# A two-layer graph attention block with a routed FFN: edge counting moved beside the first projection

## The chip, the cores and the metric

The kernel runs on one core of one Trainium2 chip. The metric is the device time of one execution in microseconds (us). Before the change the median of three runs is 1415.3 us (1413.14 to 1418.47).

## The reference, cut to what matters

```python
# x [1250, 768]; src, dst [21250], dst ascending (20000 drawn edges and 1250 self loops)
def gat(x, src, dst, W, a_src, a_dst, bias, concat):
    h = (x @ W).reshape(N, H, C)                     # layer 1: H=4, C=512; layer 2: H=1, C=768
    al_s, al_d = einsum('nhc,hc->nh', h, a_src), einsum('nhc,hc->nh', h, a_dst)
    e = leaky_relu(al_s[src] + al_d[dst], 0.2)
    ex = exp(e - segment_max(e, dst)[dst])
    alpha = ex / segment_sum(ex, dst)[dst]
    out = segment_sum(h[src] * alpha[:, :, None], dst)
    return (out.reshape(N, H * C) if concat else out.mean(axis=1)) + bias
# src, dst are the given edges followed by one more self loop per node
x = x + gat(elu(gat(layernorm(x), W1, ...)), W2, ...)
x = x + routed_ffn(layernorm(x))                     # 8 experts, top 2, and a shared expert
```

## The kernel before, in words

**Numbers.** Products are made in f16 pairs: every operand is split into a high half (ScalarE copies it to f16) and a low half (VectorE subtracts), and TensorE makes three matmuls for each product (`mm3`, L1692: high by high, high by low, low by high).

**Tiles.** The 1250 nodes are ten tiles of 125. The graph is turned into a dense matrix of counts CT [source in tile, source tile, destination], f16, built by matmuls: the 21250 edges are 170 tiles of 125; for each of them a one-hot of the source's place within its tile (OL, 125 wide) is multiplied with a one-hot of the pair of source tile and destination within a chunk of 50 destinations (OR, 500 wide, or 1000 where the tile meets two chunks). `reach[c]` is the range of edge tiles that chunk c is summed over and `met[t]` the one or two chunks that tile t meets. Since dst is ascending, a tile meets few chunks; that all edges were inside the ranges is checked at run time, and a general path, every tile by every chunk, runs if they weren't.

**Stages before the attention.** Each engine has its own program, and semaphores order them.

1. SyncE loads edges, x in three pieces (L485), W1 for head 0 (L487), a column of biases (L489), and the attention vectors (L500, L501). VectorE makes keys out of the edges (L1155 to L1161), TensorE transposes them (L1700), VectorE copies them to KEY and SLO (L1166, L1167).
2. `piece` (L1187): for a piece of x VectorE makes mean and variance (`norm`, L1174 to L1185, ScalarE the square root at L863) and normalises each tile (L1192). TensorE transposes a tile (`x_T`, L1709) into one of two pairs of banks, ScalarE and VectorE make its halves (L901, L1220), and SyncE stores them (L509), for there are three slots for ten tiles. During this stage W1's halves (L882, L1198) and the first 24 edge tiles are done. For each edge tile ScalarE subtracts (L870), VectorE compares 18 of them at once to give OL (L1229), makes OR (L1236; a ring of 8), and TensorE counts (L1722).
3. First projection, `proj(0)` on TensorE: ten tiles, beginning with tile 7 (`x_tile`), because the last three are still in their slots; the others are reloaded (L522). ScalarE makes the high half of h (`h_hi`, L888) and subtracts for more edge tiles, VectorE makes the two attention sums (L1208, twice) and the low half (L1213), and part of the 32 sums of W2's rows with the second layer's attention vectors (`v2_sums`, L1261).
4. The other 146 edge tiles. ScalarE keeps each finished chunk with its sum (L917, through four banks). Then the sum of all counts is compared with the number of edges (L1287, L1771, L1289, and a register load on VectorE and TensorE), and self loops are added to CT (L1307, L1310).
5. Masks for each of ten destination tiles: ten transposes (L1791), a scaled Relu (L1000), a store (L602), and the maximum over the sources (`chain_max`, L1331), with three tiles of the second head's projection between. `chain_shift` (L1337 to L1341) and `chain_shift_rows` (L1346) turn the maxima into rows that are stored and loaded again, broadcast.
6. The other seven tiles of the second head's projection, beside the first steps of head 0's P. A step is one source tile by one of three blocks of destinations (500, 375 and 375 wide), and takes ScalarE L929, L935, L947 and VectorE L1352, L1360, L1367; there are 30 per head.

**Attention.** A head has 15 groups: for each block the denominators (L1815) and four channel groups of 30 matmuls (L1820) in a ring of four banks. VectorE reads a group (L1405), ScalarE makes the elu's parts (L972, L973), VectorE the rest (L1412), and both the halves of H1 (L984, L1420). `al2` (L1835) sums 12 rows over a finished block. Lists say how much other work lies in each group: `CUR_STEPS` and `NEXT_STEPS` the steps of P, `PJ_STEPS` those beside the next projection, `MAX_STEPS` the maxima, `w2_at` the halves of W2's 16 chunks (L992, L1425): eight of them lie in the last head, one for each of its last eight groups, and the rest behind it, beside the second layer's first projection tile, whose matmuls wait chunk by chunk. W2's chunks come through three slots, each reloaded once its low half is made.

Of the kernel before, what the change touches and what calls it, by code (L numbers as in the profile page):

```python
# [34 lines left out]
def build(nc, x, src, dst, W1, as1, ad1, b1, W2, as2, ad2, b2, Wr, w1, w3, w2, s1, s3, s2, out):  # L35
# [33 lines left out]
    NC = N // DC  # L69
    MARGIN = 250  # L70
    KC = NT * DC
    SP = 512
    KA = ET + 1
    assert ET % 2 == 0 and KC <= SP
    reach = [(max(0, c * DC * NE // N - MARGIN) // T, min(ET, -(-((c + 1) * DC * NE // N + MARGIN) // T)))
             for c in range(NC)]
    met = [[c for c in range(NC) if reach[c][0] <= t < reach[c][1]] for t in range(ET)]
# [5 lines left out]
    XF = PIECES[2][0]  # L83
    T0 = 24
    assert T0 <= min(2 * OLP, reach[4][0])

# [11 lines left out]
    OL = at(o_p, [T, KA, T], F16)  # L98
# [32 lines left out]
    W1F = at(o_ct, [128, KD, C], F32)  # L131
    BS1 = at(o_ct + 12288, [T, NT, 2, 6], F32)
    MV1 = at(o_ct + 12800, [T, NT, 2], F32)
    WV = [at(o_y + 3072 * b, [128, D], F32) for b in range(6)]
    A2R = at(o_y + 18432, [128, 2, D], F32)
    VJ = at(o_y + 24576, [128, D], F32)
    assert o_y + 27648 <= o
# [56 lines left out]
    KEY = at(o_k + 2304, [T, KA], F32)  # L194
    SLO = at(o_k + 3072, [T, KA], F32)
# [14 lines left out]
    CS = small([T, NC], F32)  # L210
# [48 lines left out]
    with ctx:  # L259
# [26 lines left out]
        s_keys = sem("keys_made")  # L286
        s_var = sem("variance_made")
        s_sd = sem("deviation_made")
        s_xn = sem("x_normalised")
# [14 lines left out]
        s_slo = sem("sources_in_tile_made")  # L304
        s_od = sem("source_differences_made")
        s_ce = sem("chunk_kept")
        s_cs = sem("count_sum_steps")
# [5 lines left out]
        s_ctok = sem("counts_final")  # L313
# [107 lines left out]
        def v2_in(ch):  # L421

            return (s_w2g + s_wv)[ch % 6], 16 * (ch // 6 + 1)

        def x_tile(h, q):

            return (Q0 + q) % NT if h == 0 else q

        def x_use(h, q):

            return Q0 + NT * h + q

        def max_row(h):

            return ROWM[:, :] if 0 < h < H else ROW[:, 0, :]
# [10 lines left out]
        PJ_STEPS = [[0, 0, 0, 0, 2, 2, 2, 2, 2, 2], [1] * NT, [1] * NT]  # L446
# [33 lines left out]
        def _(sp):  # L480
# [49 lines left out]
            for i in range(NT):  # L530
                store_xt(i)
# [1541 lines left out]
```

## Time and profile before

| | |
|---|---|
| median of three runs | 1415.3 us |
| the profiled execution | 1416.0 us |
| its span | 1414.2 us |
| TensorE busy, share of the span | 1249.2 us, 88% |
| VectorE busy | 895.3 us, 63% |
| ScalarE busy | 604.5 us, 43% |
| GpSimd busy | 162.4 us, 11% |
| mean granted TensorE clock | 0.939 |
| data moved by DMA | 151.56 MB, 107 GB/s |
| first VectorE instruction, after waiting for the edges | 4.82 us |
| issue of W1 for head 0 | 4.42 us |
| first transpose for a mask | 197.43 us |
| last group of head 3, end of its matmuls | 724.9 us |

The times inside the span run from its start. An execution's own time has a small part around the span, 1.8 us here. The granted clock is a share of full speed (1.00 is 2.4 GHz, 0.50 is 1.2 GHz). A busy engine is one with an instruction in it; it need not run at its peak.

### The profile page before, as it was taken

Reading aid. Unit: us, or ns where it says so; the run is one execution under the profiler, and the core shown is the slowest. Engines: PE = TensorE matmul, PEld = TensorE weight load, DVE = VectorE, ACT = ScalarE, POOL = GpSimd, SP = SyncE. Lnnn points to the kernel's source line nnn. Section 1 sums busy time; section 2 is a strip of 40 time slices with the busy share of each in tenths; the row PEclk is TensorE's granted clock in tenths of the full one; section 3 lists DMA queues with packets and bytes.
Section 4 is the critical chain, followed back from the end, with each engine's and each line's share of the span. In section 5 each row is a group of like instructions: output and inputs, shape, how many; then the busy total and the mean of one; then the engine's idle time right before and its main releaser. Section 6 shows DMA issues by size and latency. Waiting matters only on the chain.

```text
span 1414.2 us, 18321 instructions
## 1 busy us (share of the span) xinstructions
PE 1249.2 (88%) x7084; PEld 816.2 (58%) x7084; DVE 895.3 (63%) x1764; ACT 604.5 (43%) x1122; POOL 162.4 (11%) x144
## 2 busy tenths in 40 slices
PE   3773987678799899989989999999999889999996
PEld 2441554334454455444557888888854756666664
DVE  6675987898987898789854556244577623333340
ACT  4275233555743574278731355000331134444441
POOL 1000000000000000000000000500010644444422
PEclk9796998898899899999998999999799989999999
DMA  8443015133413531330165410611400277767622
GB/s 205 164 137 128 23 56 164 28 101 107 122 55 101 136 99 50 90 103 23 52 207 164 141 59 30 179 63 34 138 19 1 75 237 190 190 175 180 168 61 30
DMA packets 71010, 151.56 MB, mean 107 GB/s; under 512 B 10789, under 2 KB 34853, under 8 KB 70298
## 3 DMA queue, kind: packets, MB, share of 16 engines
q1 hardware_dynamic: 64267, 133.13, 31.3%
q0 software_dynamic: 6656, 17.26, 6.3%
q8 instruction: 56, 0.92, 0.3%
q14 instruction: 31, 0.25, 0.1%
HBM read 117.78 MB, written 34.59 MB: 108 GB/s over the span
## 4 chain that ended last, share of the span: by engine, by line
PE 56%; DVE 20%; ACT 9%; issue 5%; DMA 5%; SPq 2%; POOL 2%; POOLq 0%; DVEq 0%; ACTq 0%
PE PS L1692 42%; PE PS L1820 9%; DVE sb L1236 3%; DVE sb L1331 3%; ACT sb L870 3%; DVE sb L1352 2%; DMA sb<-aa_d 2%; PE PS L1815 2%; DVE sb L1208 1%; DVE sb L1261 1%; SPq L500 1%; DVE sb L1367 1%; DMA sb<-in_L_gnn_W_dram 1%; DVE sb L1360 1%; DVE sb L1405 1%
## 5 line engine op out<-in xcount | busy, mean ns | idle before, releaser
L1692 PE MATMUL PS<-sb,sb 128*125 128x384 f16 (+8 forms) x4404 | 789.4, 340 | 47.1 <-DVE sb L1213 25.2
L1692 PEld LDWEIGHTS PS<-sb,sb 128*125 128x125 f16 (+3 forms) x4404 | 545.4, 130 | 277.9 <-issue 62.9
L1820 PE MATMUL PS<-sb,sb 125*128 125x375 f16 (+1 forms) x1440 | 267.0, 347 | 0.0
L1820 PEld LDWEIGHTS PS<-sb,sb 125*128 125x128 f16 x1440 | 141.9, 99 | 122.4 <-issue 13.8
L935 ACT ACTIVATE sb<-sb 125x375 f32<-125x375 f32 (+1 forms) x150 | 81.5, 544 | 125.0 <-DVE sb L1352 124.6
L1536 DVE SCALAR_TENSOR_TENSOR sb<-sb,sb 128x2304 f16<-128x2304 f32 x27 | 68.8, 2557 | 87.8 <-ACT sb L1067 87.8
L778 POOL TENSOR_TENSOR sb<-sb,sb 125x768 f32<-125x768 f32 x10 | 18.0, 1838 | 895.0 <-DMA sb<-in_x_dram 895.0
L1352 DVE SCALAR_TENSOR_TENSOR sb<-sb,sb,sb 125x375 f32<-125x375 f32 (+1 forms) x150 | 95.3, 637 | 11.3 <-ACT sb L929 11.3
L929 ACT ACTIVATE sb<-sb,sb 125x375 f32<-125x375 f32 (+1 forms) x150 | 93.7, 628 | 7.7 <-DMA sb<-aa_d 7.7
L1722 PE MATMUL PS<-sb,sb 125*125 125x500 f16 x286 | 69.0, 398 | 30.7 <-DVE sb L1236 22.2
L1367 DVE TENSOR_TENSOR sb<-sb,sb 125x375 f16<-125x375 f32 (+1 forms) x150 | 87.8, 585 | 0.1
L1360 DVE SCALAR_TENSOR_TENSOR sb<-sb,sb 125x375 f32<-125x375 f32 (+1 forms) x150 | 87.6, 584 | 0.1
L1208 DVE CUSTOM_DVE_ANT_0 sb<-PS,sb 125x512 f16<-125x512 f32 x80 | 55.3, 691 | 43.9 <-ACT sb L888 42.5
L947 ACT ACTIVATE sb<-sb 125x375 f16<-125x375 f32 (+1 forms) x150 | 81.6, 544 | 1.6 <-DVE sb L1360 1.5
L1331 DVE CUSTOM_DVE_ANT_0 sb<-sb,sb 125x1250 bf16<-125x1250 f32 x50 | 70.7, 1456 | 12.9 <-DMA sb<-al_d 4.8
L1815 PE MATMUL PS<-sb,sb 125*128 125x375 f16 (+1 forms) x240 | 48.7, 350 | 31.0 <-DVE sb L1367 31.0
L1722 PEld LDWEIGHTS PS<-sb,sb 125*125 125x125 f16 x286 | 39.0, 143 | 59.5 <-DVE sb L1236 30.5
L1236 DVE TENSOR_SCALAR sb<-sb,sb 125x1000 f16<-125x1000 f16 (+1 forms) x170 | 60.8, 429 | 10.0 <-PE PS L1722 9.9
L1085 ACT ACTIVATE sb<-sb 128x392 f16<-128x392 f32 (+2 forms) x33 | 17.7, 536 | 109.2 <-DVE sb L1557 109.2
L1666 DVE TENSOR_TENSOR sb<-PS,sb 128x588 f16<-128x588 f32 x32 | 23.9, 768 | 62.5 <-ACT sb L1107 55.0
L972 ACT ACTIVATE sb<-sb,sb 128x375 f32<-128x375 f32 (+1 forms) x48 | 30.8, 642 | 64.8 <-DVE sb L1405 64.6
L1067 ACT ACTIVATE sb<-sb 128x2304 f16<-128x2304 f32 x27 | 56.9, 2110 | 1.1 <-DMA sb<-in_L_ffn_w_dram 1.1
(182 smaller groups left out, 1048.9 us busy)
## 6 DMA issues: line engine op xcount, KB each, us to landing
sb<-in_L_ffn_w_dram SPq DMA_DIRECT2D x24, 1152.0 KB, 5.7
sb<-xt_d SPq DMA_DIRECT2D x37, 375.0 KB, 3.9
sb<-in_L_gnn_W_dram SPq DMA_DIRECT2D x32, 384.0 KB, 4.8
sb<-mask_d SPq DMA_DIRECT2D x20, 546.9 KB
sb<-h_d SPq DMA_DIRECT2D x10, 1000.0 KB, 6.1
h_d<-sb SPq DMA_DIRECT2D x16, 375.0 KB, 4.7
sb<-aa_d SPq DMA_DIRECT2D x5, 1093.8 KB
sb<-in_L_gnn_W_dram SPq DMA_DIRECT2D x18, 256.0 KB, 4.5
```

Source lines behind the costliest of these rows:

```text
L929: A(TMP[:, q % NTMP, 0:n], ROW[:, 1, lo:lo + n], ACT.Identity, bias=ALF[:, h, i:i + 1]).then_inc(s_p1, 1)
L935: A(TMP[:, q % NTMP, 0:n], TMP[:, q % NTMP, 0:n], ACT.Exp).then_inc(s_p3, 1)
L947: A(P[:, i, 0, lo:lo + n], TMP[:, q % NTMP, 0:n], ACT.Copy).then_inc(s_p5, 1)
L1236: V.tensor_scalar(OR[:, t % RO, 0:w, :], iok[:, 0:w, :], float(SP * c), KEY[:, t:t + 1], ALU.add, ALU.is_equal).then_inc(s_or, 1)
L1331: V.tensor_tensor_reduce(junk, max_row(h), mask, 1.0, 3.0 * NEG, ALU.subtract, ALU.max, MX[:, j:j + 1]).then_inc(s_mu, 1)
L1352: V.scalar_tensor_tensor(TMP[:, q % NTMP, 0:n], ROW[:, 0, lo:lo + n], AL[:, 0, h, i:i + 1], TMP[:, q % NTMP, 0:n], ALU.add, ALU.max).then_ ...
L1360: V.scalar_tensor_tensor(TMP[:, q % NTMP, 0:n], TMP[:, q % NTMP, 0:n], 1.0, CT[:, i, lo:lo + n], ALU.min, ALU.mult).then_inc(s_p4, 1)
L1367: V.tensor_tensor(P[:, i, 1, lo:lo + n], TMP[:, q % NTMP, 0:n], P[:, i, 0, lo:lo + n], ALU.subtract).then_inc(s_p6, 1)
L1692: ins = M(out_, lhs(a), rhs(b), start=first and a + b == 0, stop=last and a == 1)
L1722: ins = M(PS[0:T, c % 4, 0:KC], OL[:, t, :], OR[:, t % RO, w, :], start=t == reach[c][0], stop=t == reach[c][1] - 1)
L1815: ins = M(PS[:, t, 0:n], ones[:, :], P[:, i, part, lo:lo + n], start=i == 0 and part == 0, stop=i == NT - 1 and part == 1)
L1820: ins = M(PS[:, t, 0:n], hb[:, i, pa, 128 * c:128 * c + 128], P[:, i, pb, lo:lo + n], start=i == 0 and pa + pb == 0, stop=i == NT - 1 and ...
```

## The change

The ranges are the same but written another way, and the check on them is made on the keys at the start: two comparisons count the edges above the lower and those below the upper limit, and the two counts must add to twice the number of edges. CT is zeroed first, the self loops are added to it, and each chunk's sum starts with a matmul of the identity with CT, so that ScalarE's copy of a finished chunk holds them. x is normalised on ScalarE. Transposing, projecting and counting are interleaved: for each x tile, `CNT_A` edge tiles are counted, then `CNT_B` per period, in which masks also are made. W1 for head 0 is loaded right after the first piece of x, and W1 for head 1 whole into the same place afterwards. The order on each engine:

```diff
-    TOTAL = NE
+    TOTAL = 2 * NE
+    STATS = [(0, 2), (2, 5), (5, 7), (7, NT)]
-    OLP = -(-KA // NT)
-    Q0 = 7
+    OLP = -(-ET // NT)
-        PJ_STEPS = [[0, 0, 0, 0, 2, 2, 2, 2, 2, 2], [1] * NT, [1] * NT]
+        CNT_A = [0, 6, 8, 8, 8, 8, 8, 8, 8, 8]
+        CNT_B = [10] * NT
+        DIF_0, DIF_A, DIF_B = 8, [9, 8, 9, 8, 9, 9, 8, 9, 8, 9], [8, 9, 8, 17, 8, 9, 8, 9, 0, 0]
+        STAT_AT = {0: 1, 2: 2, 4: 3}
+        def masks_at(k):
+            def ready(j):
+                last = reach[-(-T * (j + 1) // DC) - 1][1]
+                return max(j, min(q for q in range(NT + 1) if SUM_B[q] >= last))
+            return [j for j in range(NT) if ready(j) == k]
+        PJ_STEPS = [[0, 0, 0, 2, 2, 2, 2, 2, 2, 2], [1] * NT, [1] * NT]
-        V2_H = [0, 1, 1, 2, 1, 2, 1, 2, 2, 2]
-        V2_H1 = [0, 0, 0, 3, 1, 1, 1, 1, 1, 1]
-        W2_EARLY = 8
+        V2_B = [1] * NT
+        V2_H1 = [4, 2, 2, 2, 2, 2, 2, 2, 2, 2]
+        W2_STEPS = [0, 0, 0, 0, 0, 0, 1, 1, 1, 2, 2, 2, 2, 2, 2]
...
             sync:
-            sp.dma_start(W1F[:, :, :], W1[:, 0:C] ...)      # after all of x
+                if n == 0:
+                    sp.dma_start(W1F[:, :, :], W1[:, 0:C] ...)
+            for i in range(2):
+                store_xt(i)
+            sp.wait_ge(s_wl, KD)
+            sp.dma_start(W1F[:, :, :], W1[:, C:2 * C] ...)
+            for ch in range(5):
+                load_v2(ch)
...
+            for j in range(NT):                              # mask stores
+                ...
+                if j % 2:
+                    load_v2(5 + j // 2)
+            chain_shift(0)
+            for i in range(3, NT):
+                load_xt(1, i)
+                if i < NT - 1:
+                    load_v2(7 + i)
...
             scalar:
+            differences(DIF_0)
+            deviation(0)
+            normalise(0)
+            xt_hi(0)
+            w1_hi(0, range(KD))
+            for i in range(NT):
+                for c in chunks_at(SUM_A[max(i - 1, 0)], SUM_A[i]):
+                    keep(c)
+                if i + 1 < NT:
+                    xt_hi(i + 1)
+                if i:
+                    h_hi(0, i - 1)
+                differences(DIF_A[i])
+                if i in STAT_AT:
+                    deviation(STAT_AT[i])
+                    normalise(STAT_AT[i])
...
+            for k in range(NT):
+                if k < KD:
+                    w1_hi(1, (k,))
+                differences(DIF_B[k])
+                for c in chunks_at(SUM_B[k], SUM_B[k + 1]):
+                    keep(c)
+                for j in masks_at(k):
+                    mask(j)
...
             vector:
+            link(V.memset(CT[:, :, :], 0.0))
+            link(V.scalar_tensor_tensor(EF[:, 0, :], EG[:, 1, :], float(EC), LIN[...], ALU.mult, ALU.subtract))
+            V.tensor_scalar(EF[:, 1, :], EF[:, 0, :], float(-EC - MARGIN), None, ALU.is_gt, ALU.add,
+                            accum_out=FS[:, 0:1]).then_inc(s_cs, 1)
+            V.tensor_scalar(EF[:, 1, :], EF[:, 0, :], float(T + MARGIN), None, ALU.is_lt, ALU.add,
+                            accum_out=FS[:, 1:2]).then_inc(s_cs, 1)
-                for i in range(a, b):
-                    V.tensor_scalar(XA[:, i, :], XA[:, i, :], MV1[:, i, 0:1], SD[:, i:i + 1], ALU.subtract,
-                                    ALU.mult).then_inc(s_xn, 1)
+            xt_lo(0)
+            w1_lo(0, range(KD))
+            for i in range(NT):
+                pair_onehots(CNT_A[i])
+                if i + 1 < NT:
+                    xt_lo(i + 1)
+                if i:
+                    h_lo(0, i - 1)
+                if i in STAT_AT:
+                    stats(STAT_AT[i])
+            h_lo(0, NT - 1)
...
-            for j in range(NT):
-                chain_max(0, j)
-                if j % 3 == 2:
-                    h_lo(1, j // 3)
+            for k in range(NT):
+                pair_onehots(CNT_B[k])
+                if k < KD:
+                    w1_lo(1, (k,))
+                if k == 0:
+                    chain_row(0)
+                else:
+                    for j in masks_at(k - 1):
+                        chain_max(0, j)
+                v2_sums(V2_B[k])
...
             tensor:
+                    for w, c in enumerate(met[t]):
+                        place = PS[0:T, c % 3, 0:KC]
+                        if t == reach[c][0]:
+                            M(place.rearrange("p (i n) -> p i n", n=DC), idh[0:T, 0:T], CT[:, :, c * DC:c * DC + DC],
+                              start=True, stop=False)
+                        ins = M(place, OL[:, t, :], OR[:, t % RO, w, :], start=False, stop=t == reach[c][1] - 1)
-            for i in range(NT // 3, NT) ...                  # proj(1) with masks between
+            x_T(0)
+            for i in range(NT):
+                if i + 1 < NT:
+                    x_T(i + 1)
+                proj(0, (i,))
+                counts(CNT_A[i])
+            for k in range(NT):
+                counts(CNT_B[k])
+                if k == 0:
+                    chain_row(0)
+                for j in masks_at(k):
+                    mask_T(j)
+            for j in masks_at(NT):
+                mask_T(j)
+            proj(1, (0,))
+            chain_shift(0)
+            proj(1, range(1, NT))
```

`x_T` has one pair of banks now and waits for the previous tile's low half. In the last head `w2_at(3, g)` gives the chunks of W2 by `W2_STEPS`: one in each of groups 6 to 8, two in each of groups 9 to 14, 15 in all; SyncE's loads of them move up accordingly, five of them ahead of the load of the first H1 tile.

## Rows read from the trace of the kernel before

**Rows 1.** The page's first part: busy time by engine
```profile
PE 1249.2 (88%) x7084; PEld 816.2 (58%) x7084; DVE 895.3 (63%) x1764; ACT 604.5 (43%) x1122; POOL 162.4 (11%) x144
```

**Rows 2.** Windows: length, busy us (instructions) by engine, granted clock, DMA share, GB/s
```profile
35.00:70.00 35.00, 25.34 (x93) 15.98 (x94) 24.06 (x53) 9.35 (x19) 0.00 (x0) 0.71 0.47 159
0.00:280.00 280.00, 187.71 (x837) 113.61 (x838) 211.00 (x489) 128.11 (x315) 4.41 (x20) 0.86 0.39 115
```

**Rows 3.** Timeline, TensorE: start, us, line, shapes, count [idle before and releaser]
```profile
57.27 18.65 PE L1692 MATMUL PS<-sb,sb 128*125 128x512 f16 x72 [2.46 <-DVE sb L1198]
...
123.89 1.09 PE L1722 MATMUL PS<-sb,sb 125*125 125x500 f16 x2 [12.54 <-DVE sb L1236]
...
193.45 0.64 PE L1722 MATMUL PS<-sb,sb 125*125 125x500 f16 x2 [0.26 <-DVE sb L1236]
...
278.18 1.01 PE L1815 MATMUL PS<-sb,sb 125*128 125x500 f16 x2 [0.55 <-DVE sb L1367]
```

**Rows 4.** Groups by form, VectorE: busy us, mean ns of one
```profile
L1483 DVE MEMSET sb<- 125x1 f16 x10 | 0.6, 59 | 0.0
L1315 DVE MEMSET sb<- 128x160 uint32 x1 | 0.2, 192 | 0.0
```

**Rows 5.** Groups by form, 0 to 280 us: busy us, mean ns of one
```profile
L929 ACT ACTIVATE sb<-sb,sb 125x500 f32<-125x500 f32 x10 | 6.9, 699 | 0.0
L1229 DVE TENSOR_SCALAR sb<-sb 125x2250 f16<-125x2250 f16 x9 | 6.7, 740 | 0.9 <-ACT sb L870 0.9
L1220 DVE TENSOR_TENSOR sb<-PS,sb 128x750 f16<-128x750 f32 x10 | 9.3, 934 | 5.2 <-ACT sb L901 5.1
L1208 DVE CUSTOM_DVE_ANT_0 sb<-PS,sb 125x512 f16<-125x512 f32 x40 | 27.6, 690 | 29.6 <-ACT sb L888 28.9
L1331 DVE CUSTOM_DVE_ANT_0 sb<-sb,sb 125x1250 bf16<-125x1250 f32 x10 | 14.6, 1458 | 3.9 <-ACT sb L1000 3.2
L1261 DVE CUSTOM_DVE_ANT_0 sb<-sb,sb 128x768 f32<-128x768 f32 x32 | 30.4, 951 | 0.5
```

**Rows 6.** DMA issues: count, KB, us from issue to landing
```profile
sb<-in_L_gnn_W_dram SPq DMA_DIRECT2D x1, 1536.0 KB, 23.0
```

**Rows 7.** Timeline, TensorE: projection, counts, f32 transposes
```profile
99.57 7.96 PE L1692 MATMUL PS<-sb,sb 128*125 128x512 f16 x36 [1.62 <-DVE sb L1213]
...
186.59 6.59 PE L1722 MATMUL PS<-sb,sb 125*125 125x500 f16 x30 [0.82 <-DVE sb L1236]
...
914.80 0.80 PE L1893 MATMUL PS<-sb,sb 125*128 125x125 f32 x6
```

**Rows 8.** Timeline, VectorE: 18 pair one-hots without a wait
```profile
140.81 6.32 DVE L1236 TENSOR_SCALAR sb<-sb,sb 125x1000 f16<-125x1000 f16 x18
```

**Rows 9.** Chain that ended last, 210 to 330 us: start, us, what
```profile
221.04 4.93 DMA sb<-xt_d
...
251.76 0.71 DVE sb L1208 x2
...
259.04 0.71 DVE sb L1208 x2
```

**Rows 10.** Timeline, TensorE: a denominator in head 0
```profile
322.13 0.81 PE L1815 MATMUL PS<-sb,sb 125*128 125x375 f16 x2 [7.63 <-DVE sb L1367]
```

**Rows 11.** Timeline, VectorE's last read of head 3, then TensorE behind it
```profile
725.10 0.55 DVE L1405 TENSOR_TENSOR sb<-PS,sb 128x375 f32<-128x375 f32 x1 [0.22 <-PE PS L1820]
...
728.89 1.45 PE L1835 MATMUL PS<-sb,sb 128*12 128x375 f16 x8
...
743.84 8.71 PE L1692 MATMUL PS<-sb,sb 128*125 128x384 f16 x36 [2.13 <-DVE sb L1425]
752.48 2.34 PE L1846 MATMUL PS<-sb,sb 12*125 12x2 f32 x20
```

**Rows 12.** Timeline, a projection tile behind a gap; then one window as in rows 2
```profile
261.34 5.66 PE L1692 MATMUL PS<-sb,sb 128*125 128x512 f16 x18 [3.20 <-DVE sb L1213]
...
57.00:63.00 6.00, 5.72 (x14) 3.17 (x15) 0.22 (x1) 0.00 (x0) 0.00 (x0) 0.50 0.92 268
```

More of the change, by code:

```diff
@@ L69, in build @@
     NC = N // DC
+    EC = NE // NC
     MARGIN = 250
@@ L130, in build @@
     assert o_y + 4 * NT * D <= o
[L131 to L137, printed above, removed]
+    W1F = at(o_e, [128, KD, C], F32)
+    WV = [at(o_y + 3072 * b, [128, D], F32) for b in range(5)]
+    A2R = at(o_y + 15360, [128, 2, D], F32)
+    VJ = at(o_y + 21504, [128, D], F32)
+    assert o_y + 24576 <= o_a
     W2S = [at(o_w2s + 3072 * i, [128, 2, D], F16) for i in range(9)]
@@ L462, in w2_at @@
         def w2_at(h, g):
-            if h == H - 1 and g >= NG - W2_EARLY:
-                return range(g - NG + W2_EARLY, g - NG + W2_EARLY + 1)
+            if h == H - 1:
+                return range(sum(W2_STEPS[:g]), sum(W2_STEPS[:g + 1]))
             if h == H:
@@ L595, in _ @@
                 load_xt(1, i)
-            for ch in range(10, NCH):
-                load_v2(ch)
             for j in range(NT):
@@ L652, in _ @@
                     store_h1(NB * h - 1)
+                    for ch in range(3, 5):
+                        load_w2(ch)
                     store_h1(NB * h)
-                    for ch in range(3, 6):
+                    for ch in range(5, 8):
                         load_w2(ch)
@@ new lines, in keep, with mask @@
+            def keep(c):
+                act.wait_ge(s_cm, reach[c][1])
+                A(CT[:, :, c * DC:c * DC + DC], PS[0:T, c % 3, 0:KC].rearrange("p (i n) -> p i n", n=DC), ACT.Copy
+                  ).then_inc(s_ce, 1)
+            def mask(j):
+                act.wait_ge(s_mt, j + 1)
+                if j >= 2:
+                    act.wait_ge(s_ms[j % 2], 32 * (j // 2))
+                    act.wait_ge(s_mu, j - 1)
+                A(MSK[:, j % 2, :].rearrange("p (a i n) -> p a i n", a=2, n=T), blocks16(PH, T, 4),
+                  ACT.Relu, bias=big[:, :], scale=NEG).then_inc(s_mm, 1)
@@ L921, in p_branch @@
+            h_hi(0, NT - 1)
+            for c in chunks_at(SUM_A[NT - 1], SUM_A[NT]):
+                keep(c)
[4 more added lines that the diff above has]
+                for c in chunks_at(SUM_B[k], SUM_B[k + 1]):
+                    keep(c)
+                for j in masks_at(k):
+                    mask(j)
+            for j in masks_at(NT):
+                mask(j)
             def p_branch(h, b, i):
@@ L1429, in _ @@
                 if h + 1 < H:
-                    for i in range(NT // 3 if h == 0 else 0, NT):
+                    for i in range(NT):
                         h_lo(h + 1, i)
@@ L1702, in _, with counts @@
             ins.then_inc(s_once, 1)
+            pe.wait_ge(s_cs, 2)
+            for a in range(2):
+                ins = M(PS[:, 6, 0:1], onesf[0:85, :], FS[:, a:a + 1], start=a == 0, stop=a == 1)
+            ins.then_inc(s_once, 1)
             def x_T(i):
                 pe.wait_ge(s_xn, i + 1)
-                if i >= 2:
-                    pe.wait_ge(s_xtl, i - 1)
-                b = 6 - 2 * (i % 2)
+                if i:
+                    pe.wait_ge(s_xtl, i)
                 for k in range(KD):
-                    ins = nc.tensor.transpose(PS[:, b + k // 3, T * (k % 3):T * (k % 3) + T],
+                    ins = nc.tensor.transpose(PS[:, 4 + k // 3, T * (k % 3):T * (k % 3) + T],
                                               XA[:, i, 128 * k:128 * k + 128], idf[0:T, 0:T])
                 ins.then_inc(s_xT, 1)
-            def counts(tiles):
-                for t in tiles:
+            counted = [0]
+            def counts(n):
+                for t in range(counted[0], counted[0] + n):
                     if t % OLP == 0:
```

358 lines of the change are left out of this document (149 added, 209 removed).

## The prediction

> **What bounds the kernel now.** I read the page first, then the busy time by stretch, then TensorE's instructions in order of time. Over the whole span TensorE is busy 88% [rows 1]. That average hides the front. From 35 to 70 us it is busy for 25.3 us at a granted clock of 0.71, and in the first 280 us VectorE is busy for 211 us, more than TensorE [rows 2]. TensorE's matmuls in order of time show why neither is full: the stages run in series. The first projection starts at 57.27 us, after every x tile is transposed; the counting of 146 of the 170 edge tiles starts at 123.89 us, after a wait of 12.54 us, and its last matmuls are at 193.45 us; masks and second projection follow, and head 0's attention runs on from 278.18 us [rows 3]. What overlap wins there is real until VectorE is full.
>
> **The profiled execution** took 1416.0 us around a span of 1414.2; the median of the runs is 1415.3. I sum against 1416.0 and take the same saving off the median.
>
> **Start, up to the first projection.** Added on VectorE: zeroing the counts, 12500 f16 per partition. The nearest rows are a memset of 160 uint32 (0.192 us) and one of a single element (0.059) [rows 4]: 0.83 ns a word, so 6250 words take 5.2 us. It starts near 0.8 us, and the key arithmetic, which waits for the edges until 4.82 us, begins 1.2 us later. Bounds: nothing (if it ends before the edges come), and 6 us (12500 elements at 0.83 ns). The Trainium skill (VectorE: DVE Perf Modes, "Zero memsets can be issued as uint32 (trn2)", with the clock in its Specifications) has one cycle per element at 0.96 GHz, by my estimate 6.5 us for these words; by that the kernel would be 1.3 us slower than by the row, whose slope I take. The three small operations of the range check lie beside the key transposes, for which VectorE waits anyway: nothing, at most 1.3. The check's matmul, cast and register load, today in the 4 us between the last count (193.45) and the first mask transpose (197.4), move here; 1 us for the load remains, 1 us for the self loops. Statistics of two tiles then end at 14.2 us. ScalarE normalises now: 500 columns cost it 0.70 [rows 5], so about 0.93 for 768. The first tile is transposed and split by 18 us, W1's six pairs of halves are made by 21.9. That needs W1: today it lands 23.0 us after its issue [rows 6] at 4.4 us, with all 3.8 MB of x ahead of it, so 5.4 MB in some 26 us. With one piece of x ahead of it instead it has 2.3 MB to come, 11 us, and is there some 13 us in. Bounds: that, and 27.4 us as now, which costs 9 us. So the **first projection starts at 21.9 instead of 57.3 us.**
>
> **First projection with counts.** TensorE per tile: 3.9 us of projection (36 matmuls in 7.96), 0.8 us of transposes and eight edge tiles. The new form of the ranges gives the very same ranges (I worked both out): 286 matmuls, to which 25 are added that bring in the self loops. 129 of them fall in this stage and 182 in the next, at 0.22 us (30 in 6.59) [rows 7]. With the first tile begun at half clock (6.6 us): 28.5 + 35 + 6 + 28 = 97.5 us. VectorE has 70 pair one-hots at 0.35 (18 in 6.32 [rows 8]), five source one-hots of 0.74, nine low halves of 0.93, per tile three operations of 0.69 on the projection [rows 5], and 12 us of statistics: 69 us, so from 22.9 us it could be done at 92, and is hidden with little to spare. ScalarE has 4.7 us per tile of 8. The reload of transposed tiles within this stage goes. With a hand-off, **VectorE is free at 98.5 us.**
>
> **Rest of the counting, with the masks.** Per period of ten tiles VectorE does 3.5 us of pair one-hots, 0.4 of source ones, 0.6 of W1 (six periods), one maximum of 1.46 and its read, 1.6, and one W2 row sum of 1.0 [rows 5, 8]: 7.2 us; ten periods, lighter at both ends, are 66.3. TensorE has 18 matmuls and ten transposes (six wider-typed ones take 0.8 [rows 7]), at most 5.3 us, hidden; ScalarE 5.3 us, hidden. The chunks under a mask are kept in the period before it, so TensorE waits for no keep. If a period did wait for the last keep, as today, it would cost 1 us of ten. VectorE done at 164.8; last mask, its maximum and the shifts at 171. The shift rows need TensorE, which now has the first tile of the second projection ahead of them (3.9 us, 7.5 at half clock): 173.5. **Today maximum and shifts end at 224.6.**
>
> **What is given back.** Three tiles of the second projection and 13 of the 32 sums lay before that point and now lie behind it. Three tiles with 4, 2 and 2 sums: 14.5 us. Seven tiles: today 7.3 us each with one sum (251.76 to 259.04 [rows 9]), with two 8.3: 57.9. End at 245.9 with 14 steps of head 0 made, against 278.2 [rows 3] with 12. **Gain 32.3.** Two steps more are made; one is (7.3 - 2.1 - 1.0 - 0.5 of waiting) / 2 = 1.85 us at 500 columns, 1.45 at 375: 2.9. In head 0 TensorE stands 7.63 us until 322.13 us for VectorE's low half of P [rows 10], so VectorE's lead counts in full. 35.2.
>
> **W2's halves.** Seven more of 16 are made in the last head. Today TensorE stands 2.13 us for one at 743.84 and reaches the sums by columns at 752.48 [rows 11]; 17 us of work after 724.9 and two chunks would bring it there at 743.9. But VectorE reads the last attention group at 725.10 having waited only 0.22 us [rows 11]: it has no room. Six more chunks before that read, 0.9 us each plus ScalarE's 0.8 before some, push its last low half of H1 from 728.5 to between 734 and 737.5. TensorE's 12-row sum over it, which today starts at 728.89 [rows 11], waits there, with 14 chunks of 0.97 behind it: 749 to 755, gain 3 to loss 3. I take 0. Ends: 8.6 gained (no lag), 5 lost.
>
> **Sum**: 35.2. I take 5 off for tiles at half clock that it does not see: after a gap of 3.20 us one took 5.66 us instead of about 4 [rows 12]; three such. 30.2: 1385.8 profiled, **median 1385**. Its own range: 1372 (nothing taken off and most of W2's 8.6) to 1400 (W1 late, W2 lost).
>
> **Rivals.** (a) Everything fits and W2's wait goes too: 43 us, 1372 or less. For: ScalarE has room in both stages. Against: the read at 725.10. 0.07. (b) The first stage is paced by hand-offs. The transposes have one pair of banks where they had two, so each tile's low half must be made before the next tile, and VectorE, 69 of 74 us full, has no slack. 2 us for each of nine tiles: 1403. 0.11. (c) SyncE gives it back: loads of transposed x for the second projection queue behind loads of W2 rows that wait for sums, and such a load takes 4.93 us [rows 9]. If load, projection and sums ran in series, a tile would take 12 us, not 8.3: 26 us over seven tiles, 1411. Against: each awaited slot is freed a tile earlier. 0.07. (d) **Slower**: TensorE stays at half clock in both new stages, its work being cut into pieces. Then 14 matmuls take 5.72 us [rows 12], 0.41 each; the first stage grows by 6.7 us for nine tiles, 60 us, the second by 11 beyond its slack: 1456. It turns to a loss once 0.43 of the two stages is at half clock. Against: 30 matmuls took 6.59 us, full clock, behind a gap of 0.82 [rows 7]. The Trainium skill (TensorE: Matmul & The Clock Gate, "What's actually happening") says that the throttled state is the default and activity releases it; by that rule, the trace agrees: 0.50 granted from 57 to 63 us after idling, full later. 0.04. (e) The range check misses its total, 42500, and the general path of 25 times 170 tiles runs: milliseconds. The ranges are those by which all edges are counted today: 0.01.
>
> **Numbers.** Forecast 0.70, the others as given. A measurement of this kernel can tell about 0.5%, 7 us, from no change. Faster by more: 0.70 + 0.07 + 0.11 = 0.88; within: (c), 0.07; slower: (d) and (e), 0.05. The range leaves out (c), (d), (e) and most of (a): 1371 to 1403.
>
> **What would show it.** First projection matmul near 22 us; its tiles about 8 us apart until 98; then VectorE without idle to 165 with a period of 7.2; shifts near 171; first attention group of head 0 near 238; TensorE's wait before 322 moved to about 290; clock 1.00 from 28 to 98. Wrong: a one-hot waiting for source differences, W1 landing after 22 us, second-projection tiles over 9 us apart. A wait over 5 us before the 12-row sum behind the last head decides W2 against the change; none decides for it.

## The result and the profile after

The changed kernel takes **1367.3 us** (median of 4 runs, 1364.4 to 1368.3) where the kernel before takes 1415.4 (4 runs beside it). The ratio is 0.9655, with a 95% interval of 0.9632 to 0.9679: 48.1 us less. The prediction had the direction, and 1385 us with a range of 1371 to 1403; the time lies below that range. The profiled execution has a span of 1366.0 us, 48.2 less than before, so it stands for the median.

First the page's busy times, then the windows (columns as in [rows 2]), the first two of them the stretches of [rows 2]:

```profile
PE 1239.5 (91%) x7111; PEld 811.3 (59%) x7111; DVE 895.7 (66%) x1766; ACT 610.3 (45%) x1108; POOL 162.3 (12%) x144
```

```profile
35.00:70.00 35.00, 34.21 (x176) 22.77 (x175) 32.34 (x87) 23.54 (x58) 0.00 (x0) 1.00 0.26 97
0.00:280.00 280.00, 216.17 (x1037) 128.46 (x1038) 253.17 (x568) 157.81 (x348) 4.46 (x20) 0.95 0.41 118
...
0.00:98.50 98.50, 79.19 (x377) 52.27 (x377) 84.75 (x207) 59.33 (x145) 4.46 (x20) 1.00 0.53 146
98.50:167.00 68.50, 51.68 (x299) 32.13 (x299) 64.43 (x153) 46.93 (x108) 0.00 (x0) 1.00 0.34 102
167.00:240.00 73.00, 52.17 (x199) 27.98 (x198) 64.20 (x138) 29.76 (x52) 0.00 (x0) 0.84 0.37 111
```

The work of the whole kernel is the same (VectorE 895.7 us against 895.3 [rows 1]). What moved is when: in the first 280 us VectorE is busy 42 us longer and TensorE 28 us longer than before. From 35 to 70 us, where TensorE had 25.3 us of work at a clock of 0.71 [rows 2], it has 34.2 at full clock.

TensorE in order of time, to be laid beside [rows 3] and [rows 10]:

```profile
23.63 6.55 PE L1727 MATMUL PS<-sb,sb 128*125 128x512 f16 x18 [2.03 <-DVE sb L1240]
...
163.84 4.05 PE L1727 MATMUL PS<-sb,sb 128*125 128x512 f16 x18
167.73 0.27 PE L1807 MATMUL PS<-sb,sb 125*20 125x125 f32 x1
...
178.87 13.52 PE L1727 MATMUL PS<-sb,sb 128*125 128x512 f16 x54 [3.09 <-DMA sb<-xt_d]
195.06 5.76 PE L1727 MATMUL PS<-sb,sb 128*125 128x512 f16 x18 [2.68 <-DVE sb L1254]
203.34 4.07 PE L1727 MATMUL PS<-sb,sb 128*125 128x512 f16 x18 [2.52 <-DVE sb L1254]
211.61 6.42 PE L1727 MATMUL PS<-sb,sb 128*125 128x512 f16 x18 [4.21 <-DVE sb L1254]
219.88 4.07 PE L1727 MATMUL PS<-sb,sb 128*125 128x512 f16 x18 [1.85 <-DVE sb L1254]
...
235.85 0.37 PE L1803 MATMUL PS<-sb,sb 125*10 125x125 f32 x1 [1.62 <-DVE sb L1254]
236.01 27.57 PE L1864 MATMUL PS<-sb,sb 125*128 125x500 f16 x120
...
268.44 0.49 PE L1859 MATMUL PS<-sb,sb 125*128 125x375 f16 x2 [1.99 <-DVE sb L1395]
...
278.60 0.38 PE L1807 MATMUL PS<-sb,sb 125*20 125x125 f32 x1 [4.89 <-DVE sb L1368]
...
322.12 7.93 PE L1727 MATMUL PS<-sb,sb 128*125 128x512 f16 x36
```

(L1727 is the projection, L1864 the attention groups, L1859 the denominators, L1807 the transpose of the shifts, L1803 that of the attention sums.) The first projection starts at 23.63 us instead of 57.27, head 0's attention at 236.0 instead of 279.2, and head 0 ends, at the next projection, at 322.1 instead of 370.4. That is the whole gain: 48.3 us. From there to the end of head 3's groups it is 355.1 us (354.5 before); from that to the sums by columns 26.9 (27.6 before, [rows 11] from 724.9 to 752.48); and 661.9 from there to the end (661.7 before).

Milestones of all runs, each from the TensorE timeline of its profiled execution, in us. "Shift rows" is the start of TensorE's transpose of the shifts, an "end" the start of the next stage's matmuls, and "columns" the start of the sums by columns less the end of head 3.

```
                         first  shift   head-0    head-0  head-3  columns  span
                         proj.  rows    attention end     end
before                   57.3   224.8   279.2     370.4   724.9   27.6     1414.2
after                    23.6   167.7   236.0     322.1   677.2   26.9     1366.0
e1  12 steps             23.6   168.3   239.1     330.4   684.6   27.9     1371.6
e12 13 steps             23.6   169.0   239.9     331.5   684.4   27.5     1374.5
e13 14, four at last     23.6   167.8   239.6     324.9   679.9   29.0     1370.5
e10 16 steps             23.6   168.1   237.5     322.4   678.0   27.6     1369.4
e2  before, 14 steps     57.5   225.1   279.6     364.7   720.8   28.9     1408.6
e3  W2 as before         23.6   168.0   236.2     322.3   677.2   26.1     1366.8
e4  late row sum         23.6   167.9   236.2     322.7   678.0   20.0     1358.8
e5  W1 last              33.9   178.4   244.7     330.9   687.1   25.5     1371.4
e6  GpSimd zeroes        21.3   168.0   234.6     320.7   676.2   27.3     1365.5
e9  e6, vectors early    21.3   165.7   233.9     320.4   675.4   27.4     1363.6
e7  x tile first         23.6   168.7   234.3     320.4   675.7   27.1     1365.1
e8  e4 + e6 + e7         21.3   167.3   232.9     319.1   674.5   19.2     1352.9
e11 e4 + e7 + e9         21.3   165.5   231.2     317.3   673.4   19.2     1352.3
```

No run edits what TensorE does behind the sums by columns, and that stretch takes 658.8 to 663.8 us. So a span can differ from another by some 5 us for nothing that an edit did, and the milestones say more than the last column.

### The profile page after: what moved, and what is told of

Read it like the earlier page. It is cut to its first block, busy times and chain, and to the rows that moved or that the text cites. A ratio compares the mean times of both kernels' runs of the same rounds, so it can differ in the third digit from the quotient of the medians.

```text
span 1366.0 us, 18379 instructions
## 1 busy us (share of the span) xinstructions
PE 1239.5 (91%) x7111; PEld 811.3 (59%) x7111; DVE 895.7 (66%) x1766; ACT 610.3 (45%) x1108; POOL 162.3 (12%) x144
## 4 chain that ended last, share of the span: by engine, by line
PE 51%; DVE 27%; ACT 8%; issue 7%; DMA 4%; POOL 2%; SPq 0%; POOLq 0%; DVEq 0%; ACTq 0%
PE PS L1727 44%; DVE sb L1359 4%; DVE sb L1380 3%; DVE sb L1278 3%; DVE sb L1395 2%; DVE sb L1388 2%; PE PS L1864 2%; DVE sb L1440 2%; DVE sb L1429 2%; DVE sb L1331 2%; DVE sb L1249 1%; PE PS L1769 1%; DVE sb L1447 1%; ACT sb L991 1%; ACT sb L981 1%
## 5 line engine op out<-in xcount | busy, mean ns | idle before, releaser
L1727 PE MATMUL PS<-sb,sb 128*125 128x384 f16 (+8 forms) x4404 | 784.6, 338 | 42.3 <-DVE sb L1254 23.7
L1727 PEld LDWEIGHTS PS<-sb,sb 128*125 128x125 f16 (+3 forms) x4404 | 541.8, 129 | 269.9 <-issue 59.8
L1864 PE MATMUL PS<-sb,sb 125*128 125x375 f16 (+1 forms) x1440 | 267.2, 347 | 0.0
L1864 PEld LDWEIGHTS PS<-sb,sb 125*128 125x128 f16 x1440 | 141.9, 99 | 122.0 <-issue 13.7
L991 ACT ACTIVATE sb<-sb 125x375 f16<-125x375 f32 (+1 forms) x150 | 81.6, 544 | 1.6 <-DVE sb L1388 1.5
L1859 PE MATMUL PS<-sb,sb 125*128 125x375 f16 (+1 forms) x240 | 47.8, 349 | 19.5 <-DVE sb L1395 19.5
L1155 ACT ACTIVATE sb<-PS,sb 98x768 f32<-98x768 f32 x32 | 28.8, 900 | 66.8 <-PE PS L1727 66.8
```

The costliest lines, as they stand in the source:

```text
L991: A(P[:, i, 0, lo:lo + n], TMP[:, q % NTMP, 0:n], ACT.Copy).then_inc(s_p5, 1)
L1727: ins = M(out_, lhs(a), rhs(b), start=first and a + b == 0, stop=last and a == 1)
L1864: ins = M(PS[:, t, 0:n], hb[:, i, pa, 128 * c:128 * c + 128], P[:, i, pb, lo:lo + n], start=i == 0 and pa + pb == 0, stop=i == NT - 1 and ...
```

## The experiments

### Are two steps of P worth 2.9 us? Runs e1 and e2

The prediction priced the two steps that are made earlier by their own work, 2.9 us. The traces pointed at more: between the last early step (278.1 before, 240.5 after) and head 0's end lie 92.3 and 81.6 us. Two runs change that one number, in either kernel.

```diff
e1_twelve_steps, in the changed kernel:
-        PJ_STEPS = [[0, 0, 0, 2, 2, 2, 2, 2, 2, 2], ...
+        PJ_STEPS = [[0, 0, 0, 0, 2, 2, 2, 2, 2, 2], ...
e2_before_fourteen, in the kernel before: the reverse
```

> The changed kernel with 12 instead of 14 steps of head 0 made before its attention (the 13th and 14th go back into head 0). Changed kernel: 1367.3 us. Theory A (the prediction's price, two steps at 1.45 each): the time rises by 3 us or less, to about 1370, and the extra gain of head 0's attention (80.3 us against 92.2 before) comes from elsewhere. Theory B (two steps more let the last low half of block 1 fall one attention group earlier, ahead of the last maxima and the shifts): a whole group is lost, 8 to 12 us, 1375 to 1379, and TensorE's wait of some 7 us for VectorE's low half of P is back, at about 286 us. If VectorE's earlier lead alone did it, the wait does not come back and the time is 1368.

> The kernel before with 14 instead of 12 steps of head 0 made beside the second projection, one number changed, nothing else of the change. Kernel before: 1415.4 us. Theory A (each step is worth its own work, and here it is only moved from the attention into the projection): between 3 us gained and nothing, 1412 to 1415. Theory B (the step that crosses an attention group's boundary counts): the wait of 7.63 us at 322 is gone and the time falls by 7 to 10 us, 1405 to 1408; that would be a part of the change's gain that needs none of its new counting.

**Measured**: e1 1371.7 us (ratio 0.9697, 0.9675 to 0.9719), 4.4 above the changed kernel; e2 1413.2 us (0.9985, 0.9969 to 1.0001), at most 4.4 us below before. By end-to-end time theory B is not borne out: e1 lies between the two theories, and e2 inside theory A's range (1412 to 1415) and not clear of no change. The traces tell more. TensorE in head 0 of e1:

```profile
239.13 26.75 PE L1864 MATMUL PS<-sb,sb 125*128 125x500 f16 x120
...
270.46 0.49 PE L1859 MATMUL PS<-sb,sb 125*128 125x375 f16 x2 [2.35 <-DVE sb L1395]
273.69 0.81 PE L1859 MATMUL PS<-sb,sb 125*128 125x375 f16 x2 [2.74 <-DVE sb L1395]
282.13 0.81 PE L1859 MATMUL PS<-sb,sb 125*128 125x375 f16 x2 [7.63 <-DVE sb L1395]
...
309.40 0.49 PE L1859 MATMUL PS<-sb,sb 125*128 125x375 f16 x2 [0.77 <-DVE sb L1395]
...
330.42 7.94 PE L1727 MATMUL PS<-sb,sb 128*125 128x512 f16 x36
```

VectorE's last low half of block 1 and its four maxima; in e1 the last of the four, then the low half:

```profile
278.28 1.46 DVE L1359 CUSTOM_DVE_ANT_0 sb<-sb,sb 125x1250 bf16<-125x1250 f32 x1
...
281.53 0.54 DVE L1395 TENSOR_TENSOR sb<-sb,sb 125x375 f16<-125x375 f32 x1
```

and in the changed kernel the low half, then the first of the four:

```profile
267.84 0.55 DVE L1395 TENSOR_TENSOR sb<-sb,sb 125x375 f16<-125x375 f32 x1
...
272.12 1.46 DVE L1359 CUSTOM_DVE_ANT_0 sb<-sb,sb 125x1250 bf16<-125x1250 f32 x1
```

In e1 TensorE waits for that low half until 282.13; in the changed kernel it has it at 268.44.

In its times e1 is the kernel before, 40.0 us earlier: the wait of 7.63 us stands at 282.13 as it did at 322.13 [rows 10], and from the start of the attention to the end of the head it is 91.3 us in e1 and 91.2 before. So with 12 steps the change gains 40.0 us at head 0's end, and the two steps bring the other 8.3 there: nearly three times their price. In the kernel before they bring 5.7 at the same place (370.4 to 364.7):

```profile
279.64 26.82 PE L1820 MATMUL PS<-sb,sb 125*128 125x500 f16 x120
...
321.21 0.38 PE L1761 MATMUL PS<-sb,sb 125*20 125x125 f32 x1 [4.89 <-DVE sb L1340]
...
364.73 7.93 PE L1692 MATMUL PS<-sb,sb 128*125 128x512 f16 x36
```

The wait of 7.63 us is gone there too, and one of 4.89 us for the shifts has come, as in the changed kernel. What the profiled runs gain at head 0's end is larger than what the medians show at the end. In e2 the 5.7 us are 4.1 at head 3's end and 2.8 at the sums by columns (749.7 for 752.5); TensorE's next wait, for VectorE in the projection behind head 0, has grown from 7.22 us to 8.36. Its median is 2.2 us less, in runs that spread from 1406.9 to 1418.4; of the 5.6 us less span, 2.8 lie behind the columns, in code that the edit doesn't touch. In e1 the 8.3 us are still 8.4 at the columns, and 4.4 in the medians. The intervals of the changed kernel and of e1 overlap slightly, so the times alone can't tell 8.3 us from 2.9: the price at head 0's end is the traces'.

### A staircase, and how many stairs: e12, e10, e13

```diff
-        PJ_STEPS = [[0, 0, 0, 2, 2, 2, 2, 2, 2, 2], ...
+        PJ_STEPS = [[0, 0, 0, 1, 2, 2, 2, 2, 2, 2], ...       # e12_thirteen_steps
+        PJ_STEPS = [[0, 0, 2, 2, 2, 2, 2, 2, 2, 2], ...       # e10_sixteen_steps
+        PJ_STEPS = [[0, 0, 0, 0, 2, 2, 2, 2, 2, 4], ...       # e13_four_at_last
```

> The changed kernel with 13 steps of head 0 made ahead of its attention (one beside the fourth tile). 14 steps gave 1367.3 us and head 0's end at 322.1, 12 steps 1371.7 and 330.4. Theory B (a staircase: what counts is whether block 1's last low half comes before the last four maxima, 1.38 us each, and the shifts): with 13 it is the ninth step inside the attention, the last one ahead of the maxima, at about 271, and TensorE waits next for the shifts at 278 in any case: head 0 ends at 322 to 323, 1367 to 1368 us. Theory A (each step carries a price of its own, half of 8.3 at head 0's end): 326, 1369.5.

> The changed kernel with 16 steps of head 0 made ahead of its attention (two beside the third tile). Theory B (staircase): TensorE's wait of 1.99 us at 268.44 goes, that for the shifts (4.89 us at 278.60), which come after the maxima, does not: at most 1 us gained, 1366 to 1369. Theory A (price per step, 2 to 4 us each at head 0's end): head 0 ends at 314 to 318, 1361 to 1365. Rival: the third tile has no shift rows to work with yet, and VectorE and TensorE wait for them there: 1368 to 1371.

**Measured**: e12 1376.2 us (0.9708, 0.9686 to 0.9731), no better than 12 steps, and against both expectations; e10 1366.0 us (0.9650, 0.9628 to 0.9672), no different from 14, as theory B had it. TensorE in e12:

```profile
239.85 27.81 PE L1864 MATMUL PS<-sb,sb 125*128 125x500 f16 x120
...
275.48 0.81 PE L1859 MATMUL PS<-sb,sb 125*128 125x375 f16 x2 [2.74 <-DVE sb L1395]
276.08 6.25 PE L1864 MATMUL PS<-sb,sb 125*128 125x375 f16 x30
...
304.65 0.49 PE L1859 MATMUL PS<-sb,sb 125*128 125x375 f16 x2 [3.29 <-DVE sb L1395]
306.03 0.81 PE L1859 MATMUL PS<-sb,sb 125*128 125x375 f16 x2 [0.89 <-DVE sb L1395]
308.28 0.81 PE L1859 MATMUL PS<-sb,sb 125*128 125x375 f16 x2 [1.44 <-DVE sb L1395]
```

and in e10:

```profile
237.31 0.37 PE L1803 MATMUL PS<-sb,sb 125*10 125x125 f32 x1 [5.23 <-DVE sb L1254]
...
280.44 0.38 PE L1807 MATMUL PS<-sb,sb 125*20 125x125 f32 x1 [6.77 <-DVE sb L1368]
...
322.41 7.94 PE L1727 MATMUL PS<-sb,sb 128*125 128x512 f16 x36
```

The 7.63 us are gone in e12 as the staircase had it: block 1's last low half is there at 275.5, ahead of the four maxima. But there are two more stairs, which the expectation had left out. A block's denominators need its last low half, which is the 12th, 22nd and 32nd step. (A step's low half is made two steps after its start, so the tenth step's comes with the 12th.) With 13 steps the 12th is still made behind the tenth tile's read (attention at 239.9, with 14 at 236.0), and the 32nd comes an attention group later than with 14: TensorE, no longer held at 282, runs into it at 304 to 308 and waits 5.6 us there. In e10 all three stairs are passed, and what remains are the shifts (6.77 us), which no step brings nearer; its attention also starts 1.5 us later than with 14, behind a wait of 5.23 us.

> The changed kernel with its 14 steps laid out as before's 12 (none beside the fourth tile) and four beside the tenth instead of two. Reading of the runs with 12, 13 and 16 steps: not the work of a step counts but three boundaries, the steps at which a block's last low half of P is done (the 12th, 22nd and 32nd). The 12th then lies behind the tenth tile's read again, as with 12 steps, and the other two where 14 put them. So head 0's attention should start at 239 (14: 236.0; 12: 239.1) and head 0 end some 3 us behind the changed kernel's 322.1, at 325 to 326 (12 steps: 330.4), with 1368.5 to 1370.5 us. Rival (a step's work is what counts, wherever it is): start and end as with 14, 1367.

**Measured**: 1370.9 us (0.9678, 0.9659 to 0.9697), a few tenths beyond the expected range; the kernel before took 1417.6 beside it. Its rows:

```profile
239.55 27.11 PE L1864 MATMUL PS<-sb,sb 125*128 125x500 f16 x120
...
281.41 0.38 PE L1807 MATMUL PS<-sb,sb 125*20 125x125 f32 x1 [4.89 <-DVE sb L1368]
...
324.93 7.93 PE L1727 MATMUL PS<-sb,sb 128*125 128x512 f16 x36
```

The same 14 steps, with only the first stair given up: start at 239.55, head 0's end at 324.9, as expected. In the trace that excludes the rival of work that counts wherever it is (the intervals of the times overlap), and it splits the 8.3 us. Against the changed kernel e13's attention starts 3.5 us later and head 0 ends 2.8 us later: the first stair. Against e13, e1 starts within 0.4 us and ends 5.5 us later: the second and the third together, for e13 passes both. The second by itself is e12 against e1, and it brought nothing (331.5 for 330.4), since the third took its place. The third by itself was not tried. Nor was the wait that is left: 4.89 us at 278.60, for a transpose of head 1's shifts that stands ahead of 60 attention matmuls.

### Is the W2 part worth nothing? e3 and e4

```diff
e3_w2_as_before:
-        W2_STEPS = [0, 0, 0, 0, 0, 0, 1, 1, 1, 2, 2, 2, 2, 2, 2]
+        W2_STEPS = [0, 0, 0, 0, 0, 0, 0, 1, 1, 1, 1, 1, 1, 1, 1]     # and the loads in their old order
e4_late_row_sum:
-                        if ch == 4:
+                        if ch == 10:
                             al2(NB * H - 1)
```

> The changed kernel with the part on W2 undone: one chunk's halves in each attention group of the last head from the eighth on, the rest behind the head, and the loads in their old order. The prediction took this part at 0, between 5 us lost and 8.6 gained. The traces say that from the last head's end to the sums by columns it is 26.9 us against 27.6. If the part is worth nothing: 1366 to 1369 us. If it hid a gain of its own behind the wait of 5.93 us: 1370 or more. If it costs: 1364 or less. Expected: TensorE's wait of 5.93 us ahead of the 12-row sum is gone, and one of about 2 us for a chunk of W2 is back.

> The changed kernel with TensorE's 12-row sum over the last head's low half of H1 moved from ahead of chunk 4 to ahead of chunk 10 of the second layer's first tile. If TensorE's wait of 5.93 us at 687.18 (for VectorE's low half, pushed back by the halves of W2) is a cost of the W2 part, all of it goes: 1361 to 1362 us, or up to 2 us less still if the clock does not fall after it (0.87 granted in this stretch). Rival: another wait takes its place (a chunk of W2, or ScalarE's 12 columns of sums, which are wanted sooner after it): 1365 to 1368.

**Measured**: e3 1366.0 us (0.9639, 0.9613 to 0.9666), the same as with the W2 part; e4 **1358.7 us** (0.9603, 0.9580 to 0.9625), 8.6 us less by the medians and 7.2 by the spans, at the far end of what was expected. TensorE behind head 3 in after:

```profile
677.18 4.07 PE L1727 MATMUL PS<-sb,sb 128*125 128x384 f16 x24
687.18 2.67 PE L1879 MATMUL PS<-sb,sb 128*12 128x375 f16 x8 [5.93 <-DVE sb L1455]
689.77 14.37 PE L1727 MATMUL PS<-sb,sb 128*125 128x384 f16 x84
704.07 2.34 PE L1890 MATMUL PS<-sb,sb 12*125 12x2 f32 x20
```

in e3 (lines one lower):

```profile
681.17 1.45 PE L1878 MATMUL PS<-sb,sb 128*12 128x375 f16 x8
682.55 7.04 PE L1726 MATMUL PS<-sb,sb 128*125 128x384 f16 x42
691.92 1.19 PE L1726 MATMUL PS<-sb,sb 128*125 128x384 f16 x6 [2.33 <-DVE sb L1459]
695.21 4.52 PE L1726 MATMUL PS<-sb,sb 128*125 128x384 f16 x18 [2.10 <-DVE sb L1459]
700.21 3.14 PE L1726 MATMUL PS<-sb,sb 128*125 128x384 f16 x18 [0.48 <-DVE sb L1459]
```

and in e4, with one window:

```profile
677.96 9.91 PE L1727 MATMUL PS<-sb,sb 128*125 128x384 f16 x60
688.64 1.44 PE L1879 MATMUL PS<-sb,sb 128*12 128x375 f16 x8 [0.77 <-DVE sb L1455]
```

```profile
677.00:704.00 27.00, 26.23 (x167) 21.23 (x165) 10.95 (x16) 9.81 (x16) 0.00 (x0) 1.00 0.70 231
```

The W2 part removes three waits of 4.9 us together (e3's rows) and makes one of 5.93, behind which the 12-row sum takes 2.67 us instead of 1.44, at a granted clock of 0.87 for the stretch (1.00 in e4). Both sides of the prediction's balance were there, and it came out at nothing. The wait was not the price of the halves, though: TensorE stood for a sum that nothing wanted yet, with chunks behind it that were ready. Six chunks later it waits 0.77 us. So the W2 part brings nothing while the sum stands in its way. With the sum moved, the stretch to the columns is 6.1 us shorter than in e3 (20.0 for 26.1). In e3 the sum itself doesn't wait, so that moving it there should gain nothing and the 6.1 us be the W2 part's; no run has the late sum without the W2 part.

### The front: e5, e6, e9, e7

```diff
e5_w1_last: W1 of head 0 loaded behind all of x
-                if n == 0:
-                    sp.dma_start(W1F[:, :, :], ...)
+            sp.dma_start(W1F[:, :, :], ...)
e6_zero_on_gpsimd:
-            link(V.memset(CT[:, :, :], 0.0))
+            nc.gpsimd.memset(CT[...].bitcast(F32), 0.0).then_inc(s_ctok, 1)    # VectorE waits for it at the self loops
e9_vectors_early: e6, and the loads of AR1 for head 0 right behind W1
e7_xt_first:
+            load_xt(1, 3)
             chain_shift(0)
```

> The changed kernel with W1 of head 0 loaded behind all of x, as before, and not behind the first piece. The prediction priced this at 9 us (W1 there at 27.4, the first projection held back by as much). If so: 1371 to 1376 us, and the first projection starts near 31. Rival: the stage behind it has enough slack in VectorE and TensorE to take most of it back: under 3 us, 1368 to 1370. Second rival: x comes sooner instead, which later tiles do not need: no help, the same 9 us.

**Measured**: 1377.7 us (0.9733, 0.9707 to 0.9758), 10.4 us more by the medians and above the expected range. W1's halves begin at 29.44 us behind a wait of 10.45, the first projection at 33.86, 10.2 us late. At the shift rows it is 10.7 us, at the attention 8.7. The stages behind take back 1.5 us at most; the prediction's 9 us for this was about right.

> The changed kernel with the counts' field zeroed by GpSimd behind its constants and not by VectorE (5.27 us from 2.18 to 7.45). VectorE's key arithmetic then starts when the edges are there, 2.7 us sooner (at 4.8). If the front is a chain from the keys on: 2 to 3 us gained, 1364.5 to 1365.5. Rival: the first projection then waits for W1 (its halves began at 18.89 without a wait) or VectorE's and GpSimd's work at the same time slows both: 1367 to 1368.

**Measured**: 1367.6 us (0.9662, 0.9638 to 0.9686): nothing by the medians. GpSimd took 5.31 us, VectorE's keys started at 5.06, the first projection came at 21.31, 2.3 us sooner, and then VectorE stood:

```profile
33.69 0.69 DVE L1249 CUSTOM_DVE_ANT_0 sb<-PS,sb 125x512 f16<-125x512 f32 x1 [2.83 <-DMA sb<-in_L_gnn_att_dst_dram]
```

A rival that was not on the list: the attention vectors of head 0, three of whose four loads SyncE issues at 29 to 30 us. The shift rows are no sooner than in after (168.0 for 167.7), though head 0 ends 1.4 us sooner. So the vectors were loaded earlier:

> GpSimd zeroing the counts, as in the run before (1367.6 us: the first projection came at 21.31 instead of 23.63, and the gain was gone at 33.69, where VectorE waited 2.83 us for head 0's attention vectors, issued on SyncE at 28 to 30 behind all of x), and these vectors loaded right behind W1, ahead of the second piece of x. If that load is what took the gain: 1365 to 1365.5 us and attention of head 0 at 233.5 or earlier. Rival: the later pieces of x, each 0.45 MB later, hold up the statistics in turn, or W1 lands later: 1367 to 1369.

**Measured**: 1365.3 us (0.9638, 0.9621 to 0.9654), 2.2 below e6. The wait is gone and the shift rows come 2.3 us sooner than in e6: so far the trace bears the cause out. But the attention starts at 233.9, later than the 233.5 expected and only 0.6 us sooner than in e6, and head 0 ends only 0.3 us sooner. The intervals overlap, so the 2.2 us by the medians are not shown to be the vectors'.

> The changed kernel with SyncE issuing the load of the second projection's fourth x tile ahead of the write and read of head 0's shift rows, behind which it lay. TensorE waits 3.09 us for that tile at 178.87, and VectorE 2.57 us at 185.28. If that wait is on the path: 1364 to 1365 us. Rival: the second projection is paced by VectorE's steps and the shifts, so that the wait moves into them: 1367, with a wait for steps or shifts of its size right after; the shift rows, issued a load later, may cost 1 us.

**Measured**: 1365.6 us (0.9648, 0.9628 to 0.9667), 1.7 less, which the overlapping intervals can't tell from nothing; in the trace the attention and head 0's end each come 1.7 us sooner (234.3, 320.4). Of the wait of 3.09 us a bit more than half was on the path.

### Together: e8 and e11

> The changed kernel with three edits together: the 12-row sum ahead of chunk 10, GpSimd zeroing the counts, and the fourth x tile loaded ahead of head 0's shift rows. If all three waits are on the path and independent: 5.5 + 2.5 + 2.5, about 1357 us. If only the late sum counts, since the other two lie ahead of stages that VectorE paces: 1361 to 1362. Nothing if each wait is replaced.

> The three edits together (late 12-row sum, counts zeroed by GpSimd, the fourth x tile's load ahead of the shift rows: 1355.6 us) and the attention vectors loaded right behind W1. If the vectors' lateness is on the path: 1353 to 1354. If not, or if x is late in turn: 1355.5 to 1357.

**Measured**: e8 1355.6 us (0.9579, 0.9552 to 0.9606), e11 **1354.9 us** (0.9570, 0.9554 to 0.9585): 12.4 us below the changed kernel and 60 below the kernel before, the best of this study. e8 is about what its parts are by themselves (8.6 + 0 + 1.7 = 10.3, measured 11.7). The early vectors' 0.7 us on top lies between the two expectations and can't be told from nothing; in e11's trace head 0 ends 1.8 us sooner than in e8's.

## Why the prediction was too small

The forecast was 32.3 + 2.9 - 5 = 30.2; the trace has 48.3 at head 0's end and nothing that matters behind it.

- **Start: right.** The zeroing took 5.27 us (5.2 from the row, 0.84 ns a word). By the Trainium skill (VectorE: DVE Perf Modes, "Zero memsets can be issued as uint32 (trn2)") the prediction estimated 6.5; the measurement decides for the row. It began at 2.18 us, not 0.8, so the keys came 2.7 us late and not 1.2, and the first projection at 23.6 instead of 21.9. W1 was there in time.
- **First stage: right.** The first tile took 6.55 us (6.6 forecast; but the granted clock reads 1.00 there, so that half clock was the reason isn't shown), the tiles start 6.7 to 8.2 us apart (about 8), and VectorE is free at 98.2 (98.5). That it fits so closely is partly luck: the start came 1.7 us late, and the stage took 74.6 us and not 76.6. Rival (b), a stage paced by hand-offs, fell: the only projection waiting for a hand-off stood 0.79 us. Rival (d) fell: from the second on a tile of the first projection takes 4.05 to 4.07 us, and the granted clock is 1.00 in both new stages. The rule of the Trainium skill that it was weighed against (TensorE: Matmul & The Clock Gate, "What's actually happening"), by which activity releases the throttle, agrees with that. Rival (e) did not occur.
- **Second stage: 5.5 us better than forecast.** Shift rows at 168.0 instead of 173.5. VectorE's maxima and shifts end 3.4 us sooner (167.6 for 171), since its periods took 5.9 to 7.1 us, 6.5 on the average and not 7.2 (a maximum with its read 1.38 us and not 1.6, a row sum 0.88 and not 1.0); 2.9 us of that went into waits for the last two masks. The other 2.1 us were the tile of the second projection that was to delay the shift's transpose: TensorE did it from 163.84 to 167.7, while VectorE was still at the last maximum. The 14 steps were made at 240.5, forecast 245.9: **5.4 us** of the difference.
- **The 5 us for tiles at half clock: wrong.** There are such tiles, 5.76 and 6.42 us beside 4.07, and TensorE's granted clock is 0.84 from 167 to 240. But the tiles start 8.27 us apart whatever they take (195.06, 203.34, 211.61, 219.88), because VectorE's reads, two steps and two sums set that pace (it stands 0.58 us in a period, for ScalarE); TensorE waits 1.9 to 4.2 us before each. A slow tile only shortens the wait of the next. The allowance charged to the path what lies in an engine's idle time. **5.0 us.**
- **Two steps for 2.9 us: the step that failed most.** From the last early step to head 0's end it was 92.3 us before and 81.6 after, 10.7 less, and with 12 steps (e1) 92.4 again. The prediction saw the 7.63 us and wrote that VectorE's lead counts in full, but it priced the lead by the steps' work. What counted was which side of the four maxima (1.38 us each), of the tenth tile's read and of a later group's read the last low half of a block falls on. The wait before 322 did not move to about 290, as forecast: it went, and one of 4.89 us for the shifts came. **7.8 us** at head 0's end; in the medians e1 shows 1.5 of them (4.4 for 2.9).
- The three make 18.2 us at head 0's end; 48.3 less 30.2 is 18.1. Rival (a), 43 us or more, had the right size, and not for its reason: W2's wait did not go.
- **W2: right, 0.7 gained for 0**, with the wait where it was said to be. Right size, wrong verdict: the 5.93 us were called the price of the halves, and e4 shows that they were the price of the place of one sum.
- **Rival (c)** showed itself once, as 3.09 us at 178.87, where a load of transposed x stood behind the shift rows' store (e7: 1.7 us of it on the path), and never behind a W2 row.

## What to carry to other kernels

When work is moved ahead of a stage, don't price it by its duration: list what the consumer waits for (the last piece of each block), and look on which side of the producer's next long job that piece falls. In these traces one piece more brought nothing (13 steps) and the next one 9.4 us at head 0's end (14). Charge a slow clock, or any slow instruction, only where the engine it is on sets the pace. And where the matmuls that wait and the matmuls that are ready stand in one queue, ask first whether the waiting one is wanted yet: moving one small sum by six chunks was the largest single gain among the edits tried here.

## What the runs showed that was not expected

GpSimd zeroed 6250 words per partition in 5.31 us, and VectorE in 5.27. While GpSimd did it, VectorE's key arithmetic with two inputs from SBUF took 0.41 to 0.42 us each, as without it. The Trainium skill (SBUF — State Buffer, "Who interferes with whom") says that such VectorE instructions contend with GpSimd instructions that read SBUF and not with those that only write; the trace agrees for the writing kind, and no run here shows the other.

A 12-row sum (8 matmuls of 375 columns) took 2.67 us behind a wait of 5.93 us and 1.44 behind one of 0.77, near the ratio of the two clock levels. The stretch from head 3's end to the sums by columns became 6.9 us shorter in e4, the wait 5.2; of the remaining 1.7, this sum is 1.2.
